# Rounding the feed-forward weights by a maximum and two differences on VectorE, with the subject indices packed into the constants

## The chip, the cores and the metric

The kernel runs on one core of a Trainium2 chip. The metric is the device time of one execution in microseconds (us); lower is better. The core's engines are TensorE (PE, with its weight load PEld), VectorE (DVE), ScalarE (ACT), GpSimd (POOL) and SyncE (SP), which issues most transfers.

## The reference

```python
# x (32, 32, 256): batch, channel, time; subjects (32,) in 0..7
w = weights[subjects]; b = bias[subjects]            # (8,32,32), (8,32)
h = einsum('bct,bcd->bdt', x, w) + b[:, :, None]     # 1024 rows of 256
q = lambda w: w.astype(float8_e4m3fn).astype(float32)
gate = silu((h @ q(gate_w)) * gate_scale)            # 256 -> 768
up   =      (h @ q(up_w))   * up_scale
out  = x + ((gate * up) @ q(down_w)) * down_scale    # 768 -> 256
```

Everything is fp32. The three weight matrices have to be rounded to the grid of float8 e4m3 (three fraction bits, a fixed step below 2^-6) before they are used.

## The kernel before

**Tiling.** The 1024 rows (batch and channel) are the free dimension, in two halves `n` of 512 columns (`TOK`). Time (256) and the hidden width (768) lie on the partitions, in 2 and 6 blocks of 128. A chunk `i` of the weights holds 128 hidden columns: 512 columns of gate and up (`GU`) and 256 of down, 768 in all (`WCOL`). TensorE works in 12 steps `s`, one for each chunk and half: `gate_up(s)` makes gate and up of a chunk in eight matmuls of 512 columns, and `down(s - 2)` adds the chunk of two steps before to the output sums in four. Chunks 0 to 3 are taken half by half; the last four steps take chunks 4 and 5 of half 0, then of half 1. The last step is cut into two pieces of 256 columns. Each activation goes through TensorE as a high part (`h_hi`, `f_hi`: a cast on ScalarE) and a low part (`h_lo`, `f_lo`: a difference on VectorE, L432 and L460).

**Order.** Each engine has a queue written out by hand, and semaphores join them.

**The start.** SP loads `const_in` (condition weights, bias, scales), then `x` and the weight chunks by turns; ACT's queue loads the subject indices `subj_i`. From the constants and the bits of the subject index a tree of predicated copies on VectorE (`select(n)`, L420) picks each batch's condition weights. The result is copied into a block diagonal `cond_bd` by `place(n)`, four blocks of 32 rows spread over ScalarE (L251), GpSimd (L334) and VectorE (L427 and L438). `select(n)` starts from copies that ScalarE (L243, L245) and GpSimd (L318) make. GpSimd builds `bias_tok` (L326). TensorE runs nine warming matmuls, then for each half the bias (L531) and the condition (L540), which waits for all four blocks of that half, and goes on to `gate_up(0)`. For half 1, GpSimd places two blocks, ScalarE one and VectorE one.

**Rounding.** For a weight piece, `power` (L367) masks the exponent of `w_in` into `w_big` on VectorE; ScalarE's `big` (L237) turns it into max(power, 2^-6) times about 2^20 by a Relu with a bias column; `add_big` (L373) adds `w_big` to `w_in` and `take_big` (L379) subtracts it again into `w_q`, which leaves the rounded weight. GpSimd does the last two for chunk 1 (L353, L356), VectorE for the others.

**A step.** ScalarE's `silu_of` (L273) waits for gate; VectorE's `fuse_of` (L452) waits for up and silu; ScalarE's `round_of` (L280) makes `f_hi`; VectorE's `rest_of` (L460) makes `f_lo`. The rounding passes stand between these in the queues.

**The tail.** VectorE's `finish(n, b)` (L466) scales an output sum and adds `x_tok`; SP and ACT store it. One quarter tile (half 0, block 1, second piece) is scaled by ScalarE (L302, `y_sc`) and added by GpSimd (L361). The stores go out in six pieces; the program waits for all.

Of the kernel before, what the change touches and what calls it, by code (L numbers as in the profile page):

```python
# [13 lines left out]
P = 128  # L14


def adaln_ffn(
    nc: bass.Bass,
    x: bass.AP,
    subjects: bass.AP,  # L20
# [33 lines left out]
    EXPONENT = 0x7F800000  # L54
# [3 lines left out]
    LEAST = 2.0 ** -6  # L58
    BELOW = 1.0 - 2.0 ** -15
    SHIFT = 2.0 ** (23 - 3)  # L60
# [4 lines left out]
    CONSTS = SCALES + 2 * IC + TB  # L65
    FLAT = G
# [3 lines left out]
    with ExitStack() as ctx:  # L70
# [10 lines left out]
        subj_i = sb("subj_i", [P, G + B], I32)  # L81
# [4 lines left out]
        down_col = const_in[:, SCALES + 2 * IC:CONSTS]  # L86
# [5 lines left out]
        big_least = sb("big_least", [P, 1])  # L92
# [15 lines left out]
        y_sc = sb("y_sc", [P, TOK // LAST])  # L108
# [7 lines left out]
        bits_ps = gu[:, 1, 1, 0:BITS * G].bitcast(I32).rearrange("p (k g) -> p k g", g=G)  # L116

        subj_in = sem("subj_in")
# [8 lines left out]
        least_set = sem("least_set")  # L127
# [15 lines left out]
        quant_power = sem("quant_power")  # L143
        quant_big = sem("quant_big")
        sum_dve = sem("sum_dve")
        sum_pool = sem("sum_pool")
        quant_dve = sem("quant_dve")
        quant_pool = sem("quant_pool")
# [9 lines left out]
        y_scaled = sem("y_scaled")  # L158
        res_dve = sem("res_dve")
        res_pool = sem("res_pool")  # L160
# [5 lines left out]

        BIGS = ((0, 0, GU), (1, 0, GU), (0, GU, WCOL), (2, 0, WCOL), (1, GU, WCOL)) + tuple((i, 0, WCOL) for i in range(3, IC))
        DVE_PIECES = ((0, 0, GU), (0, GU, WCOL), (2, 0, WCOL)) + tuple((i, 0, WCOL) for i in range(3, IC))
        POOL_PIECES = ((1, 0, GU // 2), (1, GU // 2, GU), (1, GU, WCOL))
# [5 lines left out]
        def big_count(i, lo):  # L175
            return 1 + [b for b, (t, l, h) in enumerate(BIGS) if t == i and l <= lo < h][0]

        def wait_quant(eng, i, lo):

            for pieces, done in ((DVE_PIECES, quant_dve), (POOL_PIECES, quant_pool)):  # L180
                for e, (t, l, h) in enumerate(pieces):
                    if t == i and l <= lo < h:
                        eng.wait_ge(done, e + 1)
# [7 lines left out]
        def _(sp):  # L191
# [28 lines left out]
            sp.wait_ge(res_dve, 1)  # L220
            store(0, 0, TOK)
            sp.wait_ge(res_dve, 2)
            store(1, 0, TOK // 2)
            sp.wait_ge(res_dve, 3)
            store(0, TOK, 2 * TOK)
            sp.wait_ge(res_dve, 5)
            store(1, TOK + TOK // 2, 2 * TOK)
            sp.wait_ge(stored, 16 * 6)

        @block.scalar  # L230
        def _(act):
            act.dma_start(subj_i[:], subjects).then_inc(subj_in, 16)

            def big(b):
                i, lo, hi = BIGS[b]
                act.wait_ge(quant_power, b + 1)
                nc.scalar.activation(w_big[:, i, lo:hi], w_big[:, i, lo:hi], ACT.Relu, bias=big_least[:],  # L237
                                     scale=BELOW * SHIFT).then_inc(quant_big, 1)

# [18 lines left out]
            act.wait_ge(least_set, 1)  # L258
            place(0)
            high_of_h(0, 0)  # L260
            place(1)
            big(0)
# [3 lines left out]
            high_of_h(1, 1)  # L266

# [14 lines left out]
            for s in range(STEPS - 1):  # L282
                silu_of(s)
                if s == 0:
                    round_of(s)
                    big(2)
                    continue
                if s <= 3:
                    big(s + 2)
                elif s in (5, 6):  # L290
                    big(s + 1)
                elif s == STEPS - 2:
                    silu_of(s + 1, 0, PIECES[0])
                round_of(s)
# [10 lines left out]
            act.wait_ge(res_dve, 4)  # L305
# [3 lines left out]
        def _(pool):  # L309
# [5 lines left out]
            pool.wait_ge(iota_made, 2)  # L315

# [12 lines left out]

            def place(n):  # L330

                pool.wait_ge(tree_level[n], BITS)
                for j in POOL_BLOCKS[n]:
                    nc.gpsimd.tensor_copy(*block_of(n, j)).then_inc(cond_placed[n], 1)  # L334
                pool.wait_ge(cond_placed[n], J)
# [7 lines left out]
            place_bias(0)  # L343
# [15 lines left out]
            pool.wait_ge(x_tok_ld, 16)  # L359
            pool.wait_ge(y_scaled, 1)  # L360
            nc.gpsimd.tensor_tensor(res[:, 1, 0, PIECES[1]], y_sc[:], x_tok[:, 1, 0, PIECES[1]], ALU.add).then_inc(res_pool, 1)  # L361

        @block.vector
        def _(dve):
            def power(i, lo=0, hi=WCOL):
                dve.wait_ge(w_down_ld[i] if lo == GU else w_ld[i], 16)
                nc.vector.tensor_scalar(w_big[:, i, lo:hi].bitcast(U32), w_in[:, i, lo:hi].bitcast(U32), EXPONENT,  # L367
                                        0, ALU.bitwise_and, ALU.bitwise_or).then_inc(quant_power, 1)

            def add_big(e):  # L370
                i, lo, hi = DVE_PIECES[e]
                dve.wait_ge(quant_big, big_count(i, lo))
                nc.vector.tensor_tensor(w_in[:, i, lo:hi], w_in[:, i, lo:hi], w_big[:, i, lo:hi],  # L373
                                        ALU.add).then_inc(sum_dve, 1)

            def take_big(e):
                i, lo, hi = DVE_PIECES[e]
                dve.wait_ge(sum_dve, e + 1)
                nc.vector.tensor_tensor(w_q[:, i, lo:hi], w_in[:, i, lo:hi], w_big[:, i, lo:hi],  # L379
                                        ALU.subtract).then_inc(quant_dve, 1)  # L380
# [3 lines left out]
            nc.vector.memset(big_least[:], LEAST * SHIFT).then_inc(least_set, 1)  # L384
            for k in range(BITS):
# [9 lines left out]
            dve.wait_ge(subj_in, 16)  # L395
            dve.wait_ge(bit_set, BITS)
            nc.vector.tensor_tensor(bits_ps, subj_i[:, 0:G].unsqueeze(1).to_broadcast([P, BITS, G]),
                                    bit_of[:].unsqueeze(2).to_broadcast([P, BITS, G]),
                                    ALU.bitwise_and).then_inc(bits_made, 1)
            dve.wait_ge(iota_made, 2)  # L400
            nc.vector.tensor_tensor(pick_b[:], subj_i[:, FLAT:FLAT + B], iota_p[:].to_broadcast([P, B]),
                                    ALU.is_equal).then_inc(bias_pick_made, 1)
# [32 lines left out]
            power(0, 0, GU)  # L435
# [28 lines left out]

            def finish(n, b, cols=slice(0, TOK)):
                nc.vector.scalar_tensor_tensor(res[:, b, n, cols], acc[:, TB * n + b, cols], down_col[:, b:b + 1],  # L466
                                               x_tok[:, b, n, cols], ALU.mult, ALU.add).then_inc(res_dve, 1)

            for s in range(STEPS - 1):
                fuse_of(s)  # L470
                if s == 0:
                    power(0, GU, WCOL)
                    power(2)
                elif s == 1:
                    add_big(2)
                elif s == 2:
                    power(3)
                elif s == 3:
                    add_big(3)
                elif s == 4:  # L480
                    power(4)
                elif s == 5:
                    add_big(4)
                elif s == 6:
                    add_big(5)
                elif s == STEPS - 2:
                    fuse_of(s + 1, 0, PIECES[0])
                    dve.wait_ge(x_tok_ld, 16)
                    dve.wait_ge(y0_made, 1)
                    finish(0, 0)  # L490
                rest_of(s)
                if s == 0:
                    add_big(1)
                    take_big(1)
                elif s == 1:
                    power(1, GU, WCOL)
                    take_big(2)
                elif s == 3:
                    take_big(3)
                elif s == 4:  # L500
                    power(5)
                elif s == 5:
# [184 lines left out]
```

## Time and profile before

| quantity | value |
|---|---|
| median of 3 runs | 49.47 us (49.38 to 49.66) |
| profiled execution, its own time | 49.32 us |
| its span, first to last instruction | 47.5 us |
| TensorE busy | 42.5 us, 89% |
| VectorE busy | 39.4 us, 83% |
| ScalarE busy | 25.9 us, 54% |
| GpSimd busy | 9.6 us, 20% |
| TensorE clock granted | 2.4 GHz (1.0) throughout |

The span is counted from the first instruction. The profiled execution took 1.8 us more than its span, before and after the instructions. Busy time of TensorE is modelled: matmuls overlap, so a row's duration is longer than the distance to the next matmul.

### The profile page before, as it was taken

Reading aid. Unit: us, or ns where it says so; the run is one execution under the profiler, and the core shown is the slowest. Engines: PE = TensorE matmul, PEld = TensorE weight load, DVE = VectorE, ACT = ScalarE, POOL = GpSimd, SP = SyncE. Lnnn points to the kernel's source line nnn. Section 1 sums busy time; section 2 is a strip of 40 time slices with the busy share of each in tenths; the row PEclk is TensorE's granted clock in tenths of the full one; section 3 lists DMA queues with packets and bytes.
Section 4 is the critical chain, followed back from the end, with each engine's and each line's share of the span. In section 5 each row is a group of like instructions: output and inputs, shape, how many; then the busy total and the mean of one; then the engine's idle time right before and its main releaser. Section 6 shows DMA issues by size and latency. Waiting matters only on the chain.

```text
span 47.5 us, 681 instructions
## 1 busy us (share of the span) xinstructions
PE 42.5 (89%) x201; PEld 33.1 (70%) x201; DVE 39.4 (83%) x75; ACT 25.9 (54%) x44; POOL 9.6 (20%) x20
## 2 busy tenths in 40 slices
PE   1998699999999999999999999999999999999000
PEld 1332397997877888888888778888888898987000
DVE  2849899999899999899998999998658496979900
ACT  0953219973489663798139595631846678341000
POOL 3038575089600005900000000000000000006000
PEclk9999999999999999999999999999999999999999
DMA  0499999999990000000000000000000000050692
GB/s 0 106 285 334 345 379 408 400 405 403 417 386 31 0 0 0 0 0 0 14 0 0 7 0 0 0 0 0 0 0 0 0 0 7 0 221 0 209 360 94
DMA packets 3139, 5.71 MB, mean 120 GB/s; under 512 B 448, under 2 KB 1344, under 8 KB 3136
## 3 DMA queue, kind: packets, MB, share of 16 engines
q1 hardware_dynamic: 2704, 5.40, 31.2%
q10 hardware_dynamic: 432, 0.28, 1.9%
q8 instruction: 1, 0.02, 0.1%
q14 instruction: 2, 0.02, 0.1%
HBM read 4.63 MB, written 1.05 MB: 120 GB/s over the span
## 4 chain that ended last, share of the span: by engine, by line
PE 81%; DMA 5%; POOL 3%; DVE 2%; issue 1%; DVEq 1%; POOLq 0%
PE gu L567 47%; PE acc L575 23%; PE acc L540 8%; DMA const_in<-in_consts_dram 5%; PE acc L531 2%; DVE res L466 2%; POOL bias_tok L326 2%; DVEq L70 1%; POOL tree_sb L318 1%; POOL bias_r L339 1%; POOLq L342 0%; POOLq L317 0%
## 5 line engine op out<-in xcount | busy, mean ns | idle before, releaser
L567 PE MATMUL gu<-h_hi,w_q 128*128 128x512 f32 (+1 forms) x52 | 15.2, 379 | 0.0
L567 PE MATMUL gu<-h_lo,w_q 128*128 128x512 f32 (+1 forms) x52 | 15.1, 377 | 0.0
L280 ACT CAST f_hi<-fuse 128x512 fp32r<-128x512 f32 (+1 forms) x13 | 7.5, 588 | 10.0 <-DVE fuse L452 9.9
L567 PEld LDWEIGHTS gu<-h_hi,w_q 128*128 128x128 f32 x52 | 9.6, 188 | 2.1
L567 PEld LDWEIGHTS gu<-h_lo,w_q 128*128 128x128 f32 x52 | 9.4, 188 | 2.1
L460 DVE TENSOR_TENSOR f_lo<-fuse,f_hi 128x512 fp32r<-128x512 f32 (+1 forms) x13 | 8.6, 665 | 2.7 <-ACT f_hi L280 2.5
L273 ACT ACTIVATE silu<-gu,const_in 128x512 f32<-128x512 f32 (+1 forms) x13 | 8.5, 651 | 2.0 <-PE gu L567 2.0
L452 DVE SCALAR_TENSOR_TENSOR fuse<-gu,const_in,silu 128x512 f32<-128x512 f32 (+1 forms) x13 | 9.2, 707 | 0.3 <-ACT silu L273 0.2
L575 PE MATMUL acc<-f_hi,w_q 128*128 128x512 f32 (+1 forms) x26 | 8.3, 378 | 0.0
L575 PE MATMUL acc<-f_lo,w_q 128*128 128x512 f32 (+1 forms) x26 | 8.3, 381 | 0.0
L237 ACT ACTIVATE w_big<-w_big,big_least 128x768 f32<-128x768 f32 (+2 forms) x8 | 6.2, 772 | 0.5 <-DVE w_big L367 0.5
L575 PEld LDWEIGHTS acc<-f_hi,w_q 128*128 128x128 f32 x26 | 4.9, 188 | 1.0
L575 PEld LDWEIGHTS acc<-f_lo,w_q 128*128 128x128 f32 x26 | 4.9, 188 | 0.9
L361 POOL TENSOR_TENSOR res<-y_sc,x_tok 128x256 f32<-128x256 f32 x1 | 0.7, 733 | 22.8 <-ACT y_sc L302 22.8
L379 DVE TENSOR_TENSOR w_q<-w_in,w_big 128x768 fp32r<-128x768 f32 (+2 forms) x6 | 4.9, 820 | 0.1
L373 DVE TENSOR_TENSOR w_in<-w_in,w_big 128x768 f32<-128x768 f32 (+2 forms) x6 | 4.9, 816 | 0.0
L524 PE MATMUL gu<-warm 128*128 128x512 bf16 x9 | 3.6, 581 | 1.0 <-DVE warm L382 1.0
L540 PEld LDWEIGHTS acc<-cond_bd,x_sb 128*128 128x128 f32 x32 | 3.7, 192 | 0.8 <-DVE cond_bd L427 0.5
L540 PE MATMUL acc<-cond_bd,x_sb 128*128 128x128 f32 x32 | 4.1, 280 | 0.0
L353 POOL TENSOR_TENSOR w_in<-w_in,w_big 128x256 f32<-128x256 f32 x3 | 2.4, 800 | 7.1 <-ACT w_big L237 7.1
L367 DVE TENSOR_SCALAR w_big<-w_in 128x768 uint32<-128x768 uint32 (+2 forms) x8 | 3.6, 460 | 0.0
L255 ACT CAST h_hi<-acc 128x512 fp32r<-128x512 f32 x4 | 2.3, 578 | 1.7 <-PE acc L540 1.7
(34 smaller groups left out, 24.4 us busy)
## 6 DMA issues: line engine op xcount, KB each, us to landing
w_in<-in_weights_dram SPq DMA_DIRECT2D x4, 384.0 KB, 6.3
x_tok<-in_x_by_time_dram SPq DMA_DIRECT2D x1, 1024.0 KB, 9.0
x_sb<-in_x_dram SPq DMA_DIRECT2D x1, 512.0 KB, 4.5
w_in<-in_weights_dram SPq DMA_DIRECT2D x2, 256.0 KB, 4.9
x_sb<-in_x_dram SPq DMA_DIRECT2D x2, 256.0 KB, 5.1
out_dram<-res SPq DMA_DIRECT2D x2, 256.0 KB, 2.1
w_in<-in_weights_dram SPq DMA_DIRECT2D x2, 128.0 KB, 5.4
out_dram<-res SPq DMA_DIRECT2D x2, 128.0 KB, 1.9
```

The costliest lines, as they stand in the source:

```text
L237: nc.scalar.activation(w_big[:, i, lo:hi], w_big[:, i, lo:hi], ACT.Relu, bias=big_least[:], scale=BELOW * SHIFT).then_inc(quant_big, 1)
L273: nc.scalar.activation(silu[:, s % 2, cols], gu[:, (s + q) % 2, 0, cols], ACT.Silu, scale=scale_col[:, i:i + 1]).then_inc(silu_made, 1)
L280: nc.scalar.copy(f_hi[:, s % SLOTS, cols], fuse[:, s % SLOTS, cols]).then_inc(f_hi_made, 1)
L367: nc.vector.tensor_scalar(w_big[:, i, lo:hi].bitcast(U32), w_in[:, i, lo:hi].bitcast(U32), EXPONENT, 0, ALU.bitwise_and, ALU.bitwise_or).t ...
L373: nc.vector.tensor_tensor(w_in[:, i, lo:hi], w_in[:, i, lo:hi], w_big[:, i, lo:hi], ALU.add).then_inc(sum_dve, 1)
L379: nc.vector.tensor_tensor(w_q[:, i, lo:hi], w_in[:, i, lo:hi], w_big[:, i, lo:hi], ALU.subtract).then_inc(quant_dve, 1)
L452: nc.vector.scalar_tensor_tensor(fuse[:, s % SLOTS, cols], gu[:, (s + q) % 2, 1, cols], scale_col[:, IC + i:IC + i + 1], silu[:, s % 2, co ...
L460: nc.vector.tensor_tensor(f_lo[:, s % SLOTS, cols], fuse[:, s % SLOTS, cols], f_hi[:, s % SLOTS, cols].bitcast(F32), ALU.subtract).then_in ...
L524: nc.tensor.matmul(warm_ps, warm[:], warm[:].unsqueeze(1).to_broadcast([P, TOK // P, P]), start=True, stop=True)
L540: last = nc.tensor.matmul(acc[:, KC * n + k, g * P:(g + 1) * P], x_sb[:, n, k, g], cond_bd[:, n * GH + g], start=False, stop=(g == GH - 1) ...
L567: last = nc.tensor.matmul(gu[:, (s + q) % 2, part, cols], w_q[:, i, col:col + P], h[:, n, k, cols], start=(v == 0 and k == 0), stop=(v == ...
L575: return nc.tensor.matmul(acc[:, TB * n + b, cols], w_q[:, i, GU + b * P:GU + (b + 1) * P], (f_hi, f_lo)[v][:, s % SLOTS, cols], start=(i ...
```

## The change

- The rounding is done by another identity. ScalarE computes `w_big` = |w_in| x (2^20 - 4) in one Abs straight from the loaded weights; no exponent is masked. VectorE then computes `w_in` = max(w_big, LEAST) - w_in and `w_q` = max(w_big, LEAST) - w_in(new), two `scalar_tensor_tensor` instructions whose two tensor inputs both lie in SBUF. The first leaves a rounded difference, the second the rounded weight. All eight pieces go through VectorE; GpSimd rounds none.
- The subject indices travel as 40 more columns of `const_in`; the transfer of their own on ACT's queue is gone. `pick_b` is made ahead of `bits_ps`, and `bits_ps` lies in another PSUM bank.
- On ScalarE the first `big` stands ahead of `place(1)`, and `place(1)` ahead of the first cast of h. On VectorE, `place(1)` comes right behind `select(1)`, and the first rounding piece right behind `place(1)`.
- The tail's quarter tile goes to VectorE: `finish(0, 1)` is one instruction of 512 columns ahead of the last `rest_of`, and `finish(0, 0)` comes after two `rest_of`. Five stores instead of six.

```diff
-    EXPONENT = 0x7F800000
-    LEAST = 2.0 ** -6
-    BELOW = 1.0 - 2.0 ** -15
-    SHIFT = 2.0 ** (23 - 3)
+    SHIFT = 2.0 ** 20 - 4.0
+    LEAST = 1.5 * 2.0 ** 14
...
-    CONSTS = SCALES + 2 * IC + TB
-    FLAT = G
+    SUBJECTS = SCALES + 2 * IC + TB
+    FLAT = SUBJECTS + G
+    CONSTS = FLAT + B
...
-            sp.wait_ge(res_dve, 2)
-            store(1, 0, TOK // 2)
+            sp.wait_ge(res_made, 2)
+            store(1, 0, TOK)
...
-            act.dma_start(subj_i[:], subjects).then_inc(subj_in, 16)
-
-            def big(b):
-                i, lo, hi = BIGS[b]
-                act.wait_ge(quant_power, b + 1)
-                nc.scalar.activation(w_big[:, i, lo:hi], w_big[:, i, lo:hi], ACT.Relu, bias=big_least[:],
-                                     scale=BELOW * SHIFT).then_inc(quant_big, 1)
+            def big(e):
+                i, lo, hi = QUANT[e]
+                act.wait_ge(w_down_ld[i] if lo == GU else w_ld[i], 16)
+                nc.scalar.activation(w_big[:, i, lo:hi], w_in[:, i, lo:hi], ACT.Abs, scale=SHIFT).then_inc(quant_big, 1)
...
             place(0)
+            big(0)
+            place(1)
             high_of_h(0, 0)
-            place(1)
-            big(0)
             high_of_h(0, 1)
             big(1)
             high_of_h(1, 0)
             high_of_h(1, 1)
+            big(2)
...
-            act.wait_ge(y0_made, 2)
-            nc.scalar.activation(y_sc[:], acc[:, 1, PIECES[1]], ACT.Copy, scale=down_col[:, 1:2]).then_inc(y_scaled, 1)
-            act.wait_ge(res_pool, 1)
-            act.dma_start(out_rows[:, 1, TOK // 2:TOK], res[:, 1, 0, PIECES[1]]).then_inc(stored, 16)
...
-            for e, (i, lo, hi) in enumerate(POOL_PIECES):
-                pool.wait_ge(quant_big, big_count(i, lo))
-                nc.gpsimd.tensor_tensor(w_in[:, i, lo:hi], w_in[:, i, lo:hi], w_big[:, i, lo:hi],
-                                        ALU.add).then_inc(sum_pool, 1)
-                pool.wait_ge(sum_pool, e + 1)
-                nc.gpsimd.tensor_tensor(w_q[:, i, lo:hi], w_in[:, i, lo:hi], w_big[:, i, lo:hi],
-                                        ALU.subtract).then_inc(quant_pool, 1)
...
+            def rest_of_w(e):
+                i, lo, hi = QUANT[e]
+                dve.wait_ge(quant_big, e + 1)
+                nc.vector.scalar_tensor_tensor(w_in[:, i, lo:hi], w_big[:, i, lo:hi], LEAST, w_in[:, i, lo:hi],
+                                               ALU.max, ALU.subtract).then_inc(quant_rest, 1)
+
+            def round_w(e):
+                i, lo, hi = QUANT[e]
+                dve.wait_ge(quant_rest, e + 1)
+                nc.vector.scalar_tensor_tensor(w_q[:, i, lo:hi], w_big[:, i, lo:hi], LEAST, w_in[:, i, lo:hi],
+                                               ALU.max, ALU.subtract).then_inc(quant_made, 1)
...
-            power(0, 0, GU)
             dve.wait_ge(tree_level[1], BITS)
             for j in DVE_BLOCKS[1]:
                 nc.vector.tensor_copy(*block_of(1, j)).then_inc(cond_placed[1], 1)
-            power(1, 0, GU)
-            add_big(0)
-            take_big(0)
+            rest_of_w(0)
+            round_w(0)
             for n in range(HALVES):
                 for k in range(KC):
                     rest_of_h(n, k)
+            rest_of_w(1)
+            round_w(1)
...
             s = STEPS - 1
+            rest_of(s, 0, PIECES[0])
+            dve.wait_ge(x_tok_ld, 16)
+            dve.wait_ge(y0_made, 1)
+            finish(0, 0)
             fuse_of(s, 1, PIECES[1])
-            for q in range(LAST):
-                rest_of(s, q, PIECES[q])
-
-            dve.wait_ge(y_scaled, 1)
-            finish(0, 1, PIECES[0])
+            dve.wait_ge(y0_made, 2)
+            finish(0, 1)
+            rest_of(s, 1, PIECES[1])
```

In the steps, `rest_of_w` and `round_w` of pieces 2 to 7 stand in VectorE's queue: pieces 2 and 4 whole in steps 0 and 3, between `fuse_of` and `rest_of`; piece 3 in steps 1 and 2; pieces 5, 6 and 7 in steps 4, 5 and 6, with `rest_of_w` ahead of `rest_of` and `round_w` behind it.

## Rows read from the trace of the kernel before

**Rows 1.** The page's part 1: busy time, share of the span, instructions.

```profile
PE 42.5 (89%) x201; PEld 33.1 (70%) x201; DVE 39.4 (83%) x75; ACT 25.9 (54%) x44; POOL 9.6 (20%) x20
```

**Rows 2.** Chain that ended last, in order of time: start us, us, what.

```profile
0.73 2.24 DMA const_in<-in_consts_dram
...
5.82 2.02 PE acc L540 x16
...
10.23 5.61 PE gu L567 x24
...
25.18 1.86 PE gu L567 x8
...
41.56 1.96 PE acc L575 x10
...
43.55 0.75 DVE res L466
```

**Rows 3.** Timeline of the start: start us, us, engine, line, names [idle before <-releaser].

```profile
3.00 0.51 ACT L243 COPY tree_sb<-const_in 128x384 f32<-128x384 f32 x1 [0.54 <-DMA const_in<-in_consts_dram]
...
3.18 0.27 DVE L397 TENSOR_TENSOR gu<-subj_i,bit_of 128x24 int32<-128x24 int32 x1
...
3.60 0.73 DVE L420 COPY_PREDICATED tree_sb<-gu,const_in 128x512 f32<-128x512 int32 x1
...
5.25 0.47 DVE L427 COPY cond_bd<-tree_sb 32x128 f32<-32x128 f32 x2
...
7.22 0.42 DVE L367 TENSOR_SCALAR w_big<-w_in 128x512 uint32<-128x512 uint32 x1
7.45 0.68 POOL L334 COPY cond_bd<-tree_sb 32x128 f32<-32x128 f32 x2 [0.59 <-DVE tree_sb L420]
...
7.67 0.22 DVE L438 COPY cond_bd<-tree_sb 32x128 f32<-32x128 f32 x1
...
8.18 0.41 PEld L540 LDWEIGHTS acc<-cond_bd,x_sb 128*128 128x128 f32 x3 [0.30 <-POOL cond_bd L334]
```

**Rows 4.** DMA issues in two short stretches: KB each, us from issue to landing.

```profile
subj_i<-in_subjects_dram ACTq DMA_DIRECT2D x1, 20.0 KB, 2.4
...
w_in<-in_weights_dram SPq DMA_DIRECT2D x1, 256.0 KB, 4.7
```

**Rows 5.** Timeline, 18 to 20.5 us, VectorE and GpSimd side by side.

```profile
19.17 0.55 DVE L367 TENSOR_SCALAR w_big<-w_in 128x768 uint32<-128x768 uint32 x1
...
19.27 1.04 POOL L356 TENSOR_TENSOR w_q<-w_in,w_big 128x256 fp32r<-128x256 f32 x1
...
19.94 0.92 DVE L460 TENSOR_TENSOR f_lo<-fuse,f_hi 128x512 fp32r<-128x512 f32 x1 [0.22 <-ACT f_hi L280]
```

**Rows 6.** Two lines of GpSimd: ns min/median/max.

```profile
L334 POOL COPY cond_bd<-tree_sb x3: 290/311/334, 5.3 to 7.8; 32x128 f32<-32x128 f32 x3
...
L356 POOL TENSOR_TENSOR w_q<-w_in,w_big x3: 734/748/1045, 10.5 to 19.3; 128x256 fp32r<-128x256 f32 x3
```

**Rows 7.** Groups by line and shape: busy us, mean ns | idle before.

```profile
L452 DVE SCALAR_TENSOR_TENSOR fuse<-gu,const_in,silu 128x512 f32<-128x512 f32 x11 | 8.2, 747 | 0.2 <-ACT silu L273 0.2
...
L373 DVE TENSOR_TENSOR w_in<-w_in,w_big 128x512 f32<-128x512 f32 x1 | 0.7, 693 | 0.0
```

**Rows 8.** Groups on the page: the exponent masks on VectorE.

```profile
L367 DVE TENSOR_SCALAR w_big<-w_in 128x768 uint32<-128x768 uint32 (+2 forms) x8 | 3.6, 460 | 0.0
```

**Rows 9.** Timeline of VectorE: the four low parts of h.

```profile
9.76 2.48 DVE L432 TENSOR_TENSOR h_lo<-acc,h_hi 128x512 fp32r<-128x512 f32 x4
```

**Rows 10.** Timeline of the tail.

```profile
41.68 0.49 DVE L452 SCALAR_TENSOR_TENSOR fuse<-gu,const_in,silu 128x256 f32<-128x256 f32 x1
...
42.08 0.99 DVE L460 TENSOR_TENSOR f_lo<-fuse,f_hi 128x256 fp32r<-128x256 f32 x2
...
43.02 2.06 DVE L466 SCALAR_TENSOR_TENSOR res<-acc,const_in,x_tok 128x256 f32<-128x256 f32 x4
...
43.15 0.35 PE L575 MATMUL acc<-f_lo,w_q 128*128 128x256 f32 x1
```

More of the change, by code:

```diff
@@ L19, in adaln_ffn @@
     x: bass.AP,
-    subjects: bass.AP,
     consts: bass.AP,
@@ L157, in adaln_ffn @@
         y1_made = sem("y1_made")
[L158 to L160 removed]
+        res_made = sem("res_made")
         stored = sem("stored")
         block = ctx.enter_context(nc.Block())
[L167 to L169 removed]
+        QUANT = ((0, 0, GU), (1, 0, GU), (0, GU, WCOL), (2, 0, WCOL), (1, GU, WCOL)) + tuple((i, 0, WCOL) for i in range(3, IC))
         ACT_BLOCKS = ((0,), (0,))
@@ L173, in adaln_ffn @@
         DVE_BLOCKS = ((2, 3), (3,))
-        def big_count(i, lo):
-            return 1 + [b for b, (t, l, h) in enumerate(BIGS) if t == i and l <= lo < h][0]
         def wait_quant(eng, i, lo):
[L180 to L183, printed above, removed]
+            eng.wait_ge(quant_made, 1 + [e for e, (t, l, h) in enumerate(QUANT) if t == i and l <= lo < h][0])
         def block_of(n, j):
@@ L343, in _, with place @@
             place_bias(0)
+            def place(n):
+                pool.wait_ge(tree_level[n], BITS)
+                for j in POOL_BLOCKS[n]:
+                    nc.gpsimd.tensor_copy(*block_of(n, j)).then_inc(cond_placed[n], 1)
+                pool.wait_ge(cond_placed[n], J)
             pool.wait_ge(bd_zeroed, 1)
@@ L471, in _ @@
                 if s == 0:
-                    power(0, GU, WCOL)
-                    power(2)
+                    rest_of_w(2)
+                    round_w(2)
                 elif s == 1:
-                    add_big(2)
+                    rest_of_w(3)
                 elif s == 2:
-                    power(3)
+                    round_w(3)
                 elif s == 3:
[L479 to L485, printed above, removed]
+                    rest_of_w(4)
+                    round_w(4)
+                elif s in (4, 5, 6):
+                    rest_of_w(s + 1)
                 elif s == STEPS - 2:
                     fuse_of(s + 1, 0, PIECES[0])
-                    dve.wait_ge(x_tok_ld, 16)
-                    dve.wait_ge(y0_made, 1)
-                    finish(0, 0)
                 rest_of(s)
[L492 to L502, printed above, removed]
-                    take_big(4)
-                elif s == 6:
-                    take_big(5)
+                if s in (4, 5, 6):
+                    round_w(s + 1)
             s = STEPS - 1
+            rest_of(s, 0, PIECES[0])
+            dve.wait_ge(x_tok_ld, 16)
+            dve.wait_ge(y0_made, 1)
+            finish(0, 0)
             fuse_of(s, 1, PIECES[1])
-            for q in range(LAST):
-                rest_of(s, q, PIECES[q])
-            dve.wait_ge(y_scaled, 1)
-            finish(0, 1, PIECES[0])
+            dve.wait_ge(y0_made, 2)
+            finish(0, 1)
+            rest_of(s, 1, PIECES[1])
             dve.wait_ge(y1_made, 1)
@@ L653, in _layouts @@
     own = np.repeat(subjects.reshape(g, j).T, c, axis=0)
-    subj = np.concatenate([own, np.tile(subjects[None], (P, 1))], axis=1)
+    subj = np.concatenate([own, np.tile(subjects[None], (P, 1))], axis=1).astype(np.int32)
     cond_rows = np.tile(cond.transpose(1, 0, 2).reshape(c, n * d), (j, 1))
@@ L661, in _layouts @@
     scale_cols = np.concatenate([s.reshape(-1, P).T for s in scales], axis=1)
-    consts = np.concatenate([cond_rows, bias_rows, scale_cols], axis=1)
+    consts = np.concatenate([cond_rows, bias_rows, scale_cols, subj.view(np.float32)], axis=1)
     parts = [w.reshape(kc, P, ic, P).transpose(2, 1, 0, 3).reshape(ic, P, kc * P) for w in (gate, up)]
     weights = np.concatenate([*parts, down.reshape(ic, P, t)], axis=2)
-    return {"x": halves, "subjects": subj, "consts": consts, "weights": weights,
+    return {"x": halves, "consts": consts, "weights": weights,
             "x_by_time": x.reshape(b * c, t).T}
```

72 lines of the change are left out of this document (18 added, 54 removed).

## The prediction

> **What bounds the kernel now.** I read the page's busy shares first: TensorE is busy for 89% of the span, VectorE for 83% [rows 1]. Shares alone don't say which of two full engines sets the end, so the chain of waits comes next. From 5.82 us to 43.5 us it is nothing but TensorE, matmul behind matmul, and behind it three evictions on VectorE and the last stores [rows 2]. So only three places can move the time: what lets TensorE start its real work, anything that opens a hole in its stream, and the tail after it. The timeline of the start then shows what TensorE waits for. The condition of half 0 starts at 5.82, right behind VectorE's last block (5.25 + 0.47 = 5.72); that goes back through the select (3.60) to ScalarE's copy of the constants (3.00 + 0.51 = 3.51) and to their landing [rows 3]. For half 1 there is a second such point: TensorE's load waits 0.30 us for GpSimd's two blocks (7.45 + 0.68 = 8.13) and goes on at 8.18 [rows 3]. From there the stream has no hole, so a delay at 8.18 is a delay of the end.
>
> **The rounding, in the steps.** Removed from VectorE: eight masks, 3.6 us [rows 8]. Added: chunk 1's two passes, which GpSimd made before, 2 x 0.69 for 512 columns [rows 7], and half of that for the 256 of down, some 2.1 us. The new passes are `scalar_tensor_tensor` with both tensors in SBUF; no row shows that. The nearest below is the sum of two SBUF tensors, 0.69 us for 512 columns; the nearest above is the fuse, the same instruction with one tensor in PSUM, 0.75 [rows 7]. I take 0.72, and 0.98 for 768 columns at 1.0 ns a column more (the fuse takes 0.75 for 512 and 0.49 for 256 [rows 7, 10]). Instructions that don't depend on each other overlap by 0.08 (four of 0.69 take 2.48 [rows 9]). With these durations I laid VectorE's and ScalarE's queues out against TensorE's times. Chunk 1's weights are ready at 12.9; `gate_up(2)` wants them at 10.23 + 2/3 x 5.61 = 13.97 [rows 2]. In steps 4 to 6 VectorE needs 0.67 + 0.90 + 0.61 + 0.90 = 3.1 us against TensorE's 2.8, but each has a lead to spend: before, it runs ahead of need by most of a step, and after, `fuse(4)` starts some 2 us earlier than before. Chunk 3 is ready at 24.55 and wanted at 25.18 [rows 2], a slack of 0.6, the smallest; the later ones have over 2 us. So the 1.5 us that VectorE saves buy nothing, since TensorE didn't wait for it. ScalarE loses its bias column and its wait for the masks, and isn't on the path either.
>
> **The start.** The subjects landed at 0.73 + 2.4 = 3.13, later than the constants (2.97), and VectorE's first use of them is at 3.18 [rows 2 to 4]. After, that wait is gone, but the select also waits for ScalarE's copy, which ends at 3.51, so at most 0.09 us of 3.60 are to be had. Against it the constants' rows grow by 13% (20 on 151 KB) while the 20 KB beside them vanish. Between -0.1 and +0.1, I take 0.
>
> **The second half's blocks: the step that decides.** What VectorE does while GpSimd places its two blocks changes. Before: a mask until 7.64, its block at 7.67, a mask again; no instruction with two SBUF tensors until both blocks are there. After: its block right behind the select. The mask at 7.22 overlapped the select's last copy by 0.08, so the select ends at 7.30; one step behind another needs some 0.04 between them (7.64 to 7.67 [rows 3]), so the block starts at 7.35, and 0.25 behind that (the distance of the two in L427's row, 0.47 - 0.22) `rest_of_w(0)` at 7.60, since ScalarE has its input by then (the weights land at 1.64 + 4.7 = 6.34 [rows 4], the Abs ends near 7.0). Does that hurt GpSimd? The timeline at 19 us shows how the two engines stand in each other's way. GpSimd's pass of 256 columns takes 0.75 in the median, but 1.04 when it starts at 19.27 under a VectorE mask that ends at 19.72; then VectorE's low part, otherwise 0.69, takes 0.92 while that GpSimd pass runs until 20.31 [rows 5 to 7]. Both come out if one of them stands still until the other is through: GpSimd from 19.65 on for 0.66, VectorE from 20.24 on for 0.62. The block copies show it in small (0.29 to 0.33 [rows 6]). The low part has two SBUF tensors, as `rest_of_w` has. So the first GpSimd block (7.45) gets through ahead of 7.60; the second, due at 7.80, finds `rest_of_w(0)` at work until about 8.23 (7.60 + 0.72, less the 0.07 by which an instruction lets go before its end) and needs 0.2 more: 8.43 instead of 8.13. The price is **+0.30 us** on TensorE's whole stream.
>
> The Trainium skill ("SBUF — State Buffer", section "Who interferes with whom") has the rule: a VectorE instruction with two SBUF inputs contends with a GpSimd instruction that reads SBUF, and whoever issues first blocks the other wholly. The trace agrees: 1.04 us for 0.75, and 0.92 for 0.69. By the rule the sum is the same +0.30; if only the masks blocked, it would be 0.
>
> Elsewhere the same mechanism gives something back, as GpSimd is idle after 8.4 us, but in places where TensorE doesn't wait.
>
> **The tail.** TensorE reaches the last low part of block 0 at 43.15; its operand was ready at 42.08 + 0.99 = 43.07 [rows 10]. After, VectorE starts the last fuse at 41.68 as before (silu sets that), then `finish(0, 1)` at 42.08 for 0.75, and the last low part at 42.75 for 0.42: ready at 43.17, 0.1 later. That pushes `finish(1, 0)`, which stood at 43.55 waiting for this matmul, by about 0.08. Behind it nothing changes: the same 512 and twice 256 columns, the same three stores. The 256-column `finish` that ended at 43.5 [rows 10] is gone, but it stood under TensorE's work, and so did the GpSimd quarter. The store that replaces two goes out a microsecond before the last three. **+0.08**.
>
> **Sum.** 47.5 + 0.30 + 0.08 = 47.88 for the span; the profiled execution had 1.82 outside it, so 49.70, and the median of the runs lies 0.15 above the profiled one (49.47 against 49.32): **49.85 us**. A difference under 0.5% (0.25 us) can't be told from none here.
>
> **Rivals.**
> - *No block in the way* (0.31). GpSimd's copy of 32 rows slips in, or this instruction doesn't hold what the sum of two tensors holds. For it: the observed blocks are between long passes; the block copies never stood still for more than 0.04. Against it: the row of 0.92. Time 49.47 + 0.08 = 49.55.
> - *Both blocks in the way* (0.08). If `rest_of_w(0)` starts 0.1 earlier, ahead of GpSimd's first block, and `round_w(0)` gets in between the two, the second is ready at about 9.05: +0.9, 50.45.
> - *The new passes run at half speed* (0.06). No row shows two SBUF tensors in this instruction. 2 x 6 x 768 columns at another 1.0 ns each are 9.2 us more; up to 2.8 of it fits into the slack that my layout leaves ahead of chunk 5's use, the rest stops TensorE: 49.55 + 6.4, near 56. The row of 0.75 with PSUM speaks for full speed.
> - *The start comes forward* (0.05), the other side: the select was held by its own subjects rather than by ScalarE's copy, the constants land 0.1 earlier, and no block stands in the way: 0.09 + 0.1 + 0.1 before, 49.2. It decides only if all of the select's 3.60 follows VectorE's own queue.
>
> The Trainium skill ("Vector Engine (DVE) Microarchitecture Reference", "Points that are easy to get wrong") says that such an instruction with two non-bf16 SBUF sources halves the throughput, since both read ports are taken. No run here shows it; the fp32 sum of two SBUF tensors takes both ports too and has full speed, 0.69 for 512. By that page the rival of half speed would be the forecast.
>
> **How the numbers follow.** The forecast's mechanism has 0.50, the rivals 0.31, 0.08, 0.06 and 0.05. The forecast's own range is 49.7 to 50.0 (start and tail, 0.1 each way). Within 0.5% reaches to 49.72: a fifth of the forecast's cases lie there, and nearly all of the first rival's. Slower: 0.4 + 0.14 = 0.54, and 0.02 of the first rival's; same: 0.1 + 0.27 = 0.37; faster: 0.05 and a little of the first rival, 0.07. From 49.35 to 50.2 the range holds forecast and first rival, about 0.8.
>
> **What would show it.** Right: GpSimd's second copy into `cond_bd` lasts about 0.6 us in place of 0.3, and TensorE's load behind it starts near 8.5; from there the stream has no hole until the tail; the passes of 512 columns last about 0.72; the last low part ends near 43.5 (43.17 and the 0.30). Wrong: both copies at 0.3; passes of 1.2 us and TensorE waiting for `w_q`; or a first half that starts off 5.82.

## The result

| | before | changed |
|---|---|---|
| median of 5 runs | 49.51 us (49.38 to 49.66) | 49.22 us (49.15 to 49.31) |
| profiled execution, its span | 49.32 us, 47.5 us | 49.15 us, 47.4 us |
| VectorE, ScalarE, GpSimd busy | 39.4, 25.9, 9.6 us | 38.1, 25.2, 4.4 us |

The changed kernel is faster by 0.6%: ratio 0.9937, 95% interval 0.991 to 0.9964. I had forecast 49.85 us, slower, in a range from 49.35 to 50.2. All ratios leave out executions that took over 1.5% longer than the fastest of their kernel: none of these ten, some of those in the experiments.

### The profile after

First the chain that ended last, in the changed kernel (start us, us, what). It answers to [rows 2].

```profile
0.74 2.33 DMA const_in<-in_consts_dram
...
7.55 0.28 POOL cond_bd L314
...
7.89 0.67 POOL cond_bd L314
...
8.61 2.05 PE acc L478 x16
10.66 5.50 PE gu L505 x24
16.16 0.91 PE acc L513 x4
...
25.31 1.83 PE gu L505 x8
...
41.32 2.08 PE acc L513 x10
...
43.42 0.75 DVE res L418
```

The end of the path is as before: TensorE, then the evictions. But `gate_up(0)` comes later (10.66 in this view for 10.23), and a step of eight matmuls takes 1.83 us where it took 1.86, three steps 5.50 where they took 5.61. The four matmuls of `down` between two steps went from 0.94 to 0.91. So by 41.3 us the loss has turned into a lead of 0.24 us (41.32 for 41.56). The instructions on TensorE are the same ones in the same order. Something makes each of them 2% shorter, in every stretch, also late, where no other engine rounds weights.

The timeline of the start answers to [rows 3] (start us, us, engine, line, names, idle before and its releaser).

```profile
3.09 0.51 ACT L223 COPY tree_sb<-const_in 128x384 f32<-128x384 f32 x1 [1.06 <-DMA const_in<-in_consts_dram]
...
3.69 0.74 DVE L373 COPY_PREDICATED tree_sb<-gu,const_in 128x512 f32<-128x512 int32 x1
...
7.46 0.22 DVE L390 COPY cond_bd<-tree_sb 32x128 f32<-32x128 f32 x1
7.55 1.00 POOL L314 COPY cond_bd<-tree_sb 32x128 f32<-32x128 f32 x2 [0.60 <-DVE tree_sb L373]
...
7.71 0.69 DVE L329 SCALAR_TENSOR_TENSOR w_in<-w_big,w_in 128x512 f32<-128x512 f32 x1
...
8.61 1.86 PEld L478 LDWEIGHTS acc<-cond_bd,x_sb 128*128 128x128 f32 x16 [0.51 <-POOL cond_bd L314]
```

Everything up to GpSimd's first block is 0.1 us later than before (3.09 for 3.00, 7.55 for 7.45). Then GpSimd's two blocks take 1.00 us instead of 0.68, with `rest_of_w(0)` on VectorE from 7.71 on, and TensorE's condition of half 1 starts at 8.61 instead of 8.18.

The two lines that were disputed, and GpSimd's copies (ns min/median/max of the last; busy us, mean ns of the others):

```profile
L335 DVE SCALAR_TENSOR_TENSOR w_q<-w_big,w_in 128x768 fp32r<-128x768 f32 x4 | 3.8, 950 | 0.0
...
L329 DVE SCALAR_TENSOR_TENSOR w_in<-w_big,w_in 128x512 f32<-128x512 f32 x2 | 1.4, 686 | 0.0
...
L314 POOL COPY cond_bd<-tree_sb x3: 283/308/657, 5.4 to 7.9; 32x128 f32<-32x128 f32 x3
```

The passes with two SBUF tensors take 0.69 us for 512 columns and 0.95 for 768, the price of the sums that they replace [rows 7]. GpSimd's slowest block took 657 ns; before, 334 [rows 6].

The timeline of the tail answers to [rows 10].

```profile
41.47 0.48 DVE L405 SCALAR_TENSOR_TENSOR fuse<-gu,const_in,silu 128x256 f32<-128x256 f32 x1
...
41.87 0.74 DVE L418 SCALAR_TENSOR_TENSOR res<-acc,const_in,x_tok 128x512 f32<-128x512 f32 x1
...
42.53 0.42 DVE L413 TENSOR_TENSOR f_lo<-fuse,f_hi 128x256 fp32r<-128x256 f32 x1
...
43.00 0.19 PEld L513 LDWEIGHTS acc<-f_lo,w_q 128*128 128x128 f32 x1 [0.15 <-DVE f_lo L413]
...
43.42 1.53 DVE L418 SCALAR_TENSOR_TENSOR res<-acc,const_in,x_tok 128x512 f32<-128x512 f32 x3 [0.47 <-PE acc L513]
```

The last low part is ready at 42.53 + 0.42 = 42.95, TensorE's load has waited 0.15 us for it, and `finish(1, 0)` starts at 43.42 (43.55 before).

### The profile page after: what moved, and what is told of

It is laid out like the page before. It is cut to its first block, busy times and chain, and to the rows that moved or that the text cites. A ratio compares the mean times of both kernels' runs of the same rounds, so it can differ in the third digit from the quotient of the medians.

```text
span 47.4 us, 664 instructions
## 1 busy us (share of the span) xinstructions
PE 42.6 (90%) x201; PEld 33.4 (70%) x201; DVE 38.1 (81%) x70; ACT 25.2 (53%) x43; POOL 4.4 (9%) x13
## 4 chain that ended last, share of the span: by engine, by line
PE 73%; DVE 10%; DMA 5%; POOL 2%; issue 2%; ACT 1%; DVEq 1%; POOLq 0%
PE gu L505 46%; PE acc L513 23%; DVE tree_sb L373 6%; DMA const_in<-in_consts_dram 5%; PE acc L478 4%; DVE res L418 2%; POOL cond_bd L314 2%; ACT tree_sb L223 1%; DVEq L70 1%; DVE cond_bd L380 1%; DVEq L364 0%; DVEq L378 0%; POOLq L312 0%
## 5 line engine op out<-in xcount | busy, mean ns | idle before, releaser
L335 DVE SCALAR_TENSOR_TENSOR w_q<-w_big,w_in 128x768 fp32r<-128x768 f32 (+2 forms) x8 | 6.0, 754 | 0.1
L329 DVE SCALAR_TENSOR_TENSOR w_in<-w_big,w_in 128x768 f32<-128x768 f32 (+2 forms) x8 | 6.0, 748 | 0.0
L218 ACT ACTIVATE w_big<-w_in 128x768 f32<-128x768 f32 (+2 forms) x8 | 5.4, 679 | 0.3 <-DMA w_in<-in_weights_dram 0.3
L418 DVE SCALAR_TENSOR_TENSOR res<-acc,const_in,x_tok 128x512 f32<-128x512 f32 (+1 forms) x5 | 3.0, 638 | 0.5 <-PE acc L513 0.5
L462 PEld LDWEIGHTS gu<-warm 128*128 128x128 bf16 x9 | 1.2, 143 | 2.9 <-issue 1.9
L385 DVE TENSOR_TENSOR h_lo<-acc,h_hi 128x512 fp32r<-128x512 f32 x4 | 2.7, 686 | 0.3 <-ACT h_hi L235 0.2
```

The lines of the kernel that those rows point to most:

```text
L218: nc.scalar.activation(w_big[:, i, lo:hi], w_in[:, i, lo:hi], ACT.Abs, scale=SHIFT).then_inc(quant_big, 1)
L329: nc.vector.scalar_tensor_tensor(w_in[:, i, lo:hi], w_big[:, i, lo:hi], LEAST, w_in[:, i, lo:hi], ALU.max, ALU.subtract).then_inc(quant_re ...
L335: nc.vector.scalar_tensor_tensor(w_q[:, i, lo:hi], w_big[:, i, lo:hi], LEAST, w_in[:, i, lo:hi], ALU.max, ALU.subtract).then_inc(quant_mad ...
L462: nc.tensor.matmul(warm_ps, warm[:], warm[:].unsqueeze(1).to_broadcast([P, TOK // P, P]), start=True, stop=True)
```

## The experiments

Sixteen kernels ran, in four groups, each group on a chip of its own; each ratio is to the kernel before on the same chip. "One execution" stands where a kernel ran once, for its trace, and has no ratio. "Step" is the distance from one `gate_up` to the next in the timeline, 12 matmuls of 512 columns, measured over several steps in the middle.

### Is it where the tensors lie?

Two things differ on TensorE's side: what the other engines do meanwhile, and where its operands lie in SBUF. (A third theory, C below, is that chips or executions differ.) The changed kernel has dropped `big_least`, a tensor of one column, which takes 32 bytes of each partition; so everything allocated behind it, from `warm` to the `f` tensors, starts 32 bytes lower. (`subj_i` went into `const_in` without a byte's difference behind them.) The weights `w_q`, allocated ahead, are where they were.

**b_shift**, the kernel before with the changed one's places:

```diff
-        big_least = sb("big_least", [P, 1])
...
         res = sb("res", [P, TB, HALVES, TOK])
+        big_least = sb("big_least", [P, 1])
```

> The kernel before with one 1-column tensor (big_least) laid behind all others in SBUF, so that every tensor from warm to y_sc, the moving operands of TensorE among them, starts 32 bytes lower, at the addresses of the changed kernel; no instruction differs. Theory A (addresses set the distance between matmuls): a step of 12 matmuls takes 2.75 us instead of 2.80, a 512-column matmul every 0.229 us instead of 0.233, and the kernel is 0.7 us faster, ratio 0.986. Theory B (the matmul distance follows from what the other engines do, as GpSimd and VectorE now share SBUF less): step stays at 2.80 us, ratio 1.000. Theory C (the distance is a matter of the single chip or execution): no tie to this edit, the same distance as in the other kernels of this call.

**a_pad**, the changed kernel with the places of before:

```diff
         iota_p = sb("iota_p", [P, 1])
+        pad = sb("pad", [P, 1])
```

> The changed kernel with one unused 1-column tensor ahead of warm, so that every tensor from warm to x_tok starts 32 bytes higher, where the kernel before has it; no instruction differs. Theory A (addresses): step of 12 matmuls 2.80 us, about 0.7 us slower than the changed kernel, ratio to before about 1.007 (the 0.4 us lost at the start are then left alone). Theory B (other engines): step 2.75 us and ratio 0.994 as the changed kernel. Theory C: the same distance as in the other kernels of this call.

**a_again** and **b_again**, both kernels unchanged on that chip:

> The changed kernel as it is, on the same chip as the others. All theories: ratio 0.994. Theories A and B: step of 12 matmuls 2.75 us; theory C: the distance of whatever the other kernels show here. GpSimd's two blocks of half 1 again take 1.0 us together.

> The kernel before as it is, on the same chip, for its profile. Theories A and B: step of 12 matmuls 2.80 us; theory C: the same distance as the changed kernel's here. GpSimd's two blocks of half 1 take 0.68 us together.

| kernel | ratio, 95% interval | step |
|---|---|---|
| b_shift | 0.9894 (0.9831 to 0.9958) | 2.75 us |
| a_again | 0.9939 (0.9908 to 0.9969) | 2.75 |
| b_again | one execution | 2.80 |
| a_pad | 1.0082 (1.0045 to 1.0118) | 2.80 |

Theory A held in all four. B and C, which also allow the steps of b_again and a_again, are out by b_shift and a_pad. Moving tensors by 32 bytes gives the kernel before 1.1%, by the point values more than the whole change gave it (0.6%; the intervals overlap); and with the places of before, the changed kernel is 0.8% slower than before, 0.41 us of 49.6. My sum had been +0.38. Part of the chain of b_shift shows the new step on the old instructions:

```profile
10.30 5.54 PE gu L567 x24
15.84 0.91 PE acc L575 x4
16.75 1.83 PE gu L567 x8
```

The chain of a_pad shows both at once, the late start and the old step:

```profile
8.67 2.06 PE acc L479 x16
10.73 5.61 PE gu L506 x24
16.34 0.93 PE acc L514 x4
17.27 1.87 PE gu L506 x8
```

The granted clock was 0.95 in this one execution of a_pad, from 5 us on. That isn't what made its step long: the executions of a_pad at 1.0 have spans of 48.0 and 48.1 us too (but for one of 49.6), and b_again has the step of 2.80 at 1.00.

### Which of the two operands?

**a_up64** adds a second `pad` to a_pad's; **a_wq** and **b_wq** move the weights alone, in the changed kernel and in the one before:

```diff
+        iota_p = sb("iota_p", [P, 1])
         w_q = sb("w_q", [P, IC, WCOL], F32R)
         bit_of = sb("bit_of", [P, BITS], I32)
-        iota_p = sb("iota_p", [P, 1])
```

> The changed kernel with two unused 1-column tensors ahead of warm: TensorE's moving operands start 64 bytes higher, again at 32 above a multiple of 64. Theory A1 (what matters is the moving operand's address modulo 64, 32 being the good place): step of 12 matmuls 2.75 us. Theory A2 (modulo 128 or more, or the lower the address the better): 2.80 us or another value.

> The changed kernel with the 1-column iota_p laid ahead of w_q instead of behind it: the stationary weights start 32 bytes higher, at a multiple of 64, and every moving operand stays where it was. Theory A1 (the moving operand's address alone): step of 12 matmuls 2.75 us. Theory A3 (the two operands have to agree modulo 64): 2.80 us.

> The kernel before with the 1-column iota_p laid ahead of w_q: the weights start 32 bytes higher, all else stays. The same edit made the changed kernel's step slower (2.80 for 2.75 us). Theory A4 (the distance between matmuls is short where the weights' address and the moving operand's differ by 64 modulo 128): here 0 against 64, so a step of 12 matmuls takes 2.75 us and the kernel is 0.7 us faster, ratio 0.987. Theory A5 (each operand has a good place of its own, the weights 96 and the moving operand 32 modulo 128): step 2.80, ratio 1.000.

a_up64: step 2.79 us, one execution. a_wq: step 2.80, one execution. b_wq: step 2.75, ratio 0.9903 (0.9867 to 0.9939). Theory A1, that the moving operand's place alone decides, is gone with either of the first two, and so is A3, that the two agree modulo 64 (a_up64 has that). The same edit of the weights makes the changed kernel's step longer and the old one's shorter, so the distance between the two operands' places may be what counts, or each operand has a good place of its own (A5).

**grid** measures it apart from the kernel: 64 pairs of places.

```python
for i in range(8):                     # w[i] starts at 32 * i modulo 256
    for j in range(8):                 # m[j] starts at 32 * j modulo 256
        for k in range(12):
            nc.tensor.matmul(acc[:, (k // 4) % 4], w[i][:, (k % 6) * 128:(k % 6 + 1) * 128],
                             m[j][:, (k % 4) * 512:(k % 4 + 1) * 512], start=(k % 4 == 0), stop=(k % 4 == 3))
```

> None of the reference's work: only matmuls of 512 columns on constant data, 12 in a row for each of 64 pairs of a weights tensor (w_a to w_h, at 0, 32, ... 224 bytes modulo 256) and a moving tensor (m_a to m_h, the same places), the weights in the outer loop; no other engine works meanwhile. Theory A4: a run of 12 takes 2.75 us where the two places differ by 64 or 192 and 2.80 in all others (2.79 where they agree, as one kernel showed). Theory A5: 2.75 for w_d and w_h with m_b and m_f alone. If the other engines' traffic is what an address decides on, all 64 runs take the same.

TensorE's timeline in the grid, some of the eight runs on `w_e` (128 modulo 256); a run's length is the distance to the next start:

```profile
113.84 2.95 PE L57 MATMUL acc<-m_d,w_e 128*128 128x512 f32 x12
116.64 2.89 PE L57 MATMUL acc<-m_e,w_e 128*128 128x512 f32 x12
119.36 2.97 PE L57 MATMUL acc<-m_f,w_e 128*128 128x512 f32 x12
122.16 2.92 PE L57 MATMUL acc<-m_g,w_e 128*128 128x512 f32 x12
124.92 0.40 PE L57 MATMUL acc<-m_h,w_e 128*128 128x512 f32 x1
```

`m_d`: 2.80 us. `m_e`, at the same place as the weights: 2.72. `m_f`: 2.80. `m_g`, 64 bytes further: 2.76. All eight rows of the grid, by how far the moving operand lies above the weights modulo 256, in us for 12 matmuls (smallest and largest of the eight pairs; of six for distance 0, as the first run holds the engine's start and the last has no next one):

```
distance      0      32     64     96    128    160    192    224
from       2.72   2.80   2.74   2.80   2.79   2.80   2.78   2.78
to         2.75   2.81   2.76   2.82   2.80   2.82   2.80   2.80
```

Of these eight distances 0 and 64 are short, and no other, wherever the pair lies; A5 is out. Theory A4 was wrong in the second half (192 isn't short), and in expecting a long step at equal places. And no other engine works during these runs, but for 1 us of VectorE at their start: the effect needs TensorE alone.

**b_zero** and **b_192** put that to the test in the kernel itself (`pad = sb("pad", [P, 40])` and `[P, 24]` ahead of `warm`):

> The kernel before with an unused tensor of 40 columns (160 bytes) ahead of warm, so that TensorE's moving operands (h, f) and its weights start at the same place modulo 256. Theory A6, read from the grid of 64 pairs (the short distance is where the moving operand lies 0 or 64 bytes above the weights modulo 256): a step of 12 matmuls takes 2.73 to 2.75 us, ratio 0.985 to 0.990. Theory A4 as first put (64 modulo 128): 2.80 us, ratio 1.000.

> The kernel before with 96 bytes ahead of warm: the moving operands lie 192 above the weights modulo 256, which is 64 modulo 128. Theory A4 (64 modulo 128): step 2.75 us, ratio 0.990. Theory A6 (0 or 64 modulo 256): step 2.80 us, ratio 1.000.

b_zero: step 2.72 us, ratio 0.9878 (0.9831 to 0.9925). b_192: step 2.80, ratio 1.0009 (0.9972 to 1.0046). The steps of these kernels now follow from their places:

| kernel | weights, moving operand, modulo 256 | distance | step, us |
|---|---|---|---|
| before, b_again, a_pad, b_pack | 224, 64 | 96 | 2.80 |
| changed, a_again, b_shift | 224, 32 | 64 | 2.75 |
| a_up64 | 224, 96 | 128 | 2.79 |
| a_wq | 0, 32 | 32 | 2.80 |
| b_wq | 0, 64 | 64 | 2.75 |
| b_zero | 224, 224 | 0 | 2.72 |
| b_192 | 224, 160 | 192 | 2.80 |

### The held block

**a_gate**, the changed kernel with a wait:

```diff
+            dve.wait_ge(cond_placed[1], J)
             rest_of_w(0)
             round_w(0)
```

> The changed kernel with one more wait: VectorE starts the first rounding pass only when all four blocks of half 1 are placed. Theory D (GpSimd's block copy stands still while a VectorE instruction with two SBUF tensors runs): GpSimd's two copies take 0.65 us together instead of 1.00, TensorE starts the condition of half 1 near 8.3 instead of 8.6, and the kernel is 0.3 us faster than the changed one, ratio to before about 0.988. Rival E (the copies are slow for another reason, such as their place behind ScalarE's or the transfers): the copies still take 1.0 us and nothing is won, ratio 0.994. Rival F (TensorE's first gate and up then wait for w_q or h_lo, as VectorE starts 0.5 us later): start at 8.3, but a hole of 0.1 us or more ahead of the stream.

**a_act**, which gives the block away instead:

```diff
-        ACT_BLOCKS = ((0,), (0,))
-        POOL_BLOCKS = ((1,), (1, 2))
+        ACT_BLOCKS = ((0,), (0, 1))
+        POOL_BLOCKS = ((1,), (2,))
```

> The changed kernel with one of GpSimd's two blocks of half 1 given to ScalarE, so that GpSimd's one block (due at 7.55, done by 7.84) ends ahead of VectorE's first rounding pass; VectorE's queue isn't delayed. Theory D (the block stands still behind a VectorE instruction with two SBUF tensors): all blocks are there near 8.05, TensorE goes on at 8.3 without a hole instead of 8.6, and nearly all of it reaches the end, as VectorE starts when it did (the delay of 0.5 us in the run with the wait is what made holes of 0.3 us later): 0.25 to 0.3 us faster than the changed kernel, ratio 0.988. Rival G (VectorE has no slack left even so): the stream gets holes ahead of chunks 3 to 5 and half of it or less is left, ratio 0.991 to 0.994.

a_gate: ratio 0.9937 (0.9914 to 0.996), no better than the changed kernel. Its timeline and chain:

```profile
7.61 0.63 POOL L314 COPY cond_bd<-tree_sb 32x128 f32<-32x128 f32 x2 [0.60 <-DVE tree_sb L373]
...
8.27 0.69 DVE L329 SCALAR_TENSOR_TENSOR w_in<-w_big,w_in 128x512 f32<-128x512 f32 x1 [0.53 <-POOL cond_bd L314]
8.29 0.86 PEld L479 LDWEIGHTS acc<-cond_bd,x_sb 128*128 128x128 f32 x7 [0.27 <-POOL cond_bd L314]
...
10.34 5.51 PE gu L506 x24
...
19.52 1.87 PE gu L506 x8
21.39 1.07 PE acc L514 x4
...
PEld acc L514 <- DVE w_q L335: 0.3, 1, 0.3
```

The two blocks take 0.63 us again, and TensorE goes on at 8.29: theory D holds. But VectorE now starts its passes at 8.27 instead of 7.71, and the chunk 1 down weights come late for `down(2)`: that `down` takes 1.07 us instead of 0.91, and TensorE's load waited 0.3 us in all for `w_q`. From 10.34 to 43.38 the stream takes 33.04 us, in the changed kernel (10.66 to 43.40) 32.74. The 0.3 us won at the start are given back where VectorE has no slack; the hole that rival F looked for at the first step is some 10 us later.

a_act: ratio 0.9849 (0.9802 to 0.9897). Its timeline:

```profile
5.24 1.19 PE L469 MATMUL acc<-bias_tok,ones_r 128*128 128x512 f32 x2 [0.23 <-POOL bias_tok L298]
...
7.51 0.62 ACT L231 COPY cond_bd<-tree_sb 32x128 f32<-32x128 f32 x2 [1.28 <-DVE tree_sb L373]
...
7.61 0.28 POOL L314 COPY cond_bd<-tree_sb 32x128 f32<-32x128 f32 x1 [0.60 <-DVE tree_sb L373]
7.76 0.69 DVE L329 SCALAR_TENSOR_TENSOR w_in<-w_big,w_in 128x512 f32<-128x512 f32 x1
```

GpSimd's one block takes 0.28 us with the same pass running on VectorE from 7.76, as it came first. TensorE waits for none of the blocks of half 1 in this execution. But its first half is late for another reason, the 1.19 us of the bias matmuls (more on that below), so that the stream begins at 10.57 and this profile doesn't show the gain. The spans of the other executions do: 46.9 to 47.1 us, where the changed kernel's were 47.4 and 47.5. So about 0.4 us reaches the end, no less than the 0.33 that the held block had cost. The trace of a_act_zero below, without the late bias, begins its stream at 10.26.

### The tail

**a_split** is the changed kernel with `finish(0, 1)` in two pieces; **a_act_split** is the same on a_act.

```diff
-            finish(0, 1)
+            finish(0, 1, PIECES[0])
             rest_of(s, 1, PIECES[1])
+            finish(0, 1, PIECES[1])
```

> The changed kernel with finish(0, 1) in two pieces of 256 columns, one ahead of the last low part and one behind it. If the 512-column finish ahead of the last low part holds TensorE up (0.15 us at 43.0 in the changed kernel), the low part is ready 0.15 us earlier, TensorE has no hole there, and the last store goes out 0.1 us earlier: ratio to before about 0.992. Rival: the second piece then runs into finish(1, 0) and nothing is won, or the stores are the bound (their packets follow one another without a gap from 45.2 us): ratio 0.994.

> The last one together with finish(0, 1) in two pieces. Both mechanisms hold and add: 0.1 us faster than with the block alone, ratio 0.986. Rival: the stores' own train of packets bounds the tail, and the extra instruction wins nothing: ratio as with the block alone.

a_split: ratio 0.997 (0.9948 to 0.9991), a_act_split 0.987 (0.9823 to 0.9917). In a_split's profile TensorE doesn't wait for the low part and `finish(1, 0)` starts at 43.28 instead of 43.42, of which 0.06 is an earlier start of the condition (8.55 for 8.61). So the hole is real, but the time shows nothing of it: a_act_split is not faster than a_act, and a_split's times (median 49.34 us) are no shorter than the changed kernel's, though their spans (47.3 us) are. What lengthens the part outside the span there stays open.

### Packing alone, and the two repairs together

**b_pack** is the kernel before with the subjects in `const_in` and no place moved. **a_act_zero** is a_act with 192 bytes ahead of `warm`.

> The kernel before with the subject indices packed into the constants and nothing else changed; no SBUF address from w_in on moves. Theory H (the start waits for the constants, whose rows are 13% longer): the constants land and the select starts 0 to 0.1 us later, ratio 1.000 to 1.002. Rival (the wait for the subjects' own transfer was on the path, or the two transfers slowed each other): the select starts 0.1 us earlier, ratio 0.998. The step stays at 2.80 us.

> The changed kernel with GpSimd's one block given to ScalarE and the operands at the same place modulo 256, in place of 64 above. Theory A6: step of 12 no longer than 2.75 us, and if the grid's 0.01 to 0.03 us for each run of 12 between the two good places hold here, 0.1 to 0.3 us faster still: ratio 0.980 to 0.985, but VectorE has hardly any slack, so holes ahead of chunk 3 may take it back: 0.985.

b_pack: ratio 1.0031 (0.9999 to 1.0062). The constants landed after 2.34 us; in before, b_again, b_shift, b_zero and b_192 they took 2.2 to 2.5. The select started at 3.71, in before at 3.60 and in b_again, the same kernel, at 3.70. Packing wins nothing and costs 0 to 0.3 us; the profiles can't narrow it further. a_act_zero: ratio 0.9874 (0.9827 to 0.992), steps of 2.72 us, with 0.07 us lost at chunk 3 (eight matmuls in 1.88 us where its others take 1.81); it can't be told from a_act. Its load for the condition of half 1 and the start of its stream, from the timeline and the chain:

```profile
8.19 0.98 PEld L479 LDWEIGHTS acc<-cond_bd,x_sb 128*128 128x128 f32 x8 [0.16 <-ACT cond_bd L232]
...
10.26 5.46 PE gu L506 x24
```

ScalarE's second block is now the last one, and the stream begins 0.40 us earlier than in the changed kernel (10.66). Each of a_act, a_act_zero and b_zero beats the kernel before by 1.2 to 1.5%, and a_act the changed one too: its interval (0.9802 to 0.9897) ends below 0.991.

## Why the prediction was wrong

- **The step that failed** is one that I didn't cost at all: "only three places can move the time", the start, a hole in the stream, the tail; and so, in the sum, TensorE's stream stood at its old length, a change of nothing without a reason. A fourth place moved it, the distance between matmuls. It was 2% shorter, 4 to 5 ns a matmul of 512 columns, because removing `big_least` moved the operands 32 bytes. The stream began 0.43 us later (10.66 for 10.23) but took 32.74 us instead of 33.29, hole included, and so it ended 0.12 earlier. a_pad, which takes this one thing away, is at 1.0082 (1.0045 to 1.0118), or 49.9 us, by my 49.85. So near a hit is in part luck: the interval alone is 0.4 us wide.
- **The held block (+0.30)**: shown. 1.00 us for 0.68, TensorE at 8.61 for 8.18, of which 0.33 is the block; a_gate and a_act take it away. Of the two rows that I built it on, one didn't carry it: GpSimd's 1.04 us [rows 5] began under a mask, which has one SBUF tensor, and the block that began at 7.45 under such a mask took no more than 0.33 [rows 3 and 6]. The other row, 0.92 us for a low part with two SBUF tensors, and now the 657 ns do. What held that GpSimd pass, no run here shows.
- **The start (0, from -0.1 to +0.1)**: 0.09 later in the profiled execution, which is within what b_again shows of the unchanged kernel (0.10), and b_pack gives +0.15 us with an interval of 0 to 0.3. The rival in which the start comes forward is out. What I left out of the path to 5.82: GpSimd's `bias_tok` and the two bias matmuls end at 5.07 + 0.70 = 5.77, as late as VectorE's block at 5.72, and the whole chain of the kernel before runs through them. Where they take 1.19 us, they and not the select set the start of the first half.
- **The tail (+0.08)**: the wait is there, 0.15 us; the term was small by half. The low part itself ended where the sum has it, 43.17 less the 0.21 by which VectorE's last fuse came earlier (41.47 for 41.68); TensorE was a little further ahead (its high part of that block started at 42.77 for 43.03). The time doesn't resolve it.
- **The passes (0.72 for 512 columns)**: 0.69. The rival of half speed is out, and with it the sentence of the Trainium skill ("Vector Engine (DVE) Microarchitecture Reference", "Points that are easy to get wrong") that two non-bf16 SBUF sources halve this instruction: 0.69 us for 512 fp32 columns and 0.95 for 768 are 1.0 ns a column. The measurement decides.
- **The slack (chunk 3: 0.6 us)**: in the changed kernel 25.15 - 24.79, about 0.4, as the chunk was ready 0.24 later than I had laid it out (24.55); a_gate, 0.5 us later on VectorE, used it up. That the 1.5 us that VectorE saves (1.3 measured) buy nothing was right.
- **No block in the way** and **both blocks in the way**, the other rivals: out. GpSimd's first block wasn't held (0.28 us) and the second was, once (657 ns). The rule of the Trainium skill ("SBUF — State Buffer", "Who interferes with whom") agrees once more, now for this instruction too: 657 ns for 334.

## What to carry to other kernels

Where TensorE's stream sets the time, read the distance between its matmuls before and after, and not only its holes: here a tensor dropped ahead of the operands changed it by 2%, and the time by more than the edit itself. Compare an edit's two sides with all tensors at the same places (one unused tensor does it), or the edit is credited with the placement. And an engine that is freed early, as VectorE was here, starts its next work early, too: look at what shares a path with that work before you call the freed time harmless.

## What the runs showed of the hardware

- With fp32r operands, a run of 12 matmuls of 512 columns takes 2.72 to 2.76 us when the moving operand starts 0 or 64 bytes above the weights modulo 256, and 2.78 to 2.82 at the six other multiples of 32, at the same granted clock (1.0 in the grid). It is 4 to 5 ns a matmul. For matmuls of 256 columns the runs show no such rule: eight of them took 0.91 us (changed, b_shift) and 0.94 (a_again, a_act) at distance 64, 0.96 at 0 (b_zero), 0.95 at 96 (before) and 0.92 at 192 (b_192). Why the places matter, no run shows.
- GpSimd's copy of 32 rows, 0.29 us, waited for a VectorE instruction with two SBUF tensors that was at work: 0.66 us. One that had begun before that instruction wasn't held: 0.28 us in a_act.
- The first two bias matmuls took 0.70 us together in some executions (before, b_shift, a_gate, b_zero), 1.19 in others (a_again, b_again, a_act), and 0.84 to 1.17 in four more. With 1.19, the stream of the kernel before and its variants began at 10.43 (b_again), 10.56 (b_pack) and 10.72 us (b_192), where it was 10.23 in before. The granted clock shows 1.00 in both cases. It comes and goes between executions of one kernel (before and b_again), so spans of single profiles differ by 0.3 us without cause in the kernel. In a_again it hides the held block: TensorE's load for half 1 waits for no block there. Why it happens stays open.
